# Three groups of instructions moved in a fused attention and experts kernel: the residual into y, half of the scores, a bias centring

## The chip, the cores and the metric

The kernel runs on one core of a Trainium2 chip. The metric is the device time of one execution in microseconds (us). Each engine (TensorE or PE, VectorE or DVE, ScalarE or ACT, GpSimd or Pool, SyncE or SP) has its own list of instructions, written out by hand, which it runs in that order; semaphores tie the lists together.

## What is computed

Input x is 4 sequences of 32 tokens by 256 features, 128 tokens in all. Three stages follow, each on a layer-normed x and each added back to x:

```
x = x + xattn(layernorm(x), ctx)     # cross attention, 16 heads of 16, causal, context of 64 features
x = x + attn(layernorm(x))           # self attention, 16 heads of 16, q/k/v/o = x W + b + 0.5 (x B) A
x = x + ffn(layernorm(x))            # mixture of experts

def attn:  scores = q k / 4;  p = softmax(scores);  out = lora_linear(p v, Wo, bo, Bo, Ao)
def ffn:   logits = x @ router_w.T;  s = sqrt(softplus(logits))
           4 best of 32 experts by s + expert_bias, weights s / sum(s)
           out = sum over the experts of weight * (silu(clip(x wg)) * clip(x wu)) @ wd, + one shared expert
```

All 32 experts are computed for all 128 tokens, and the router's weights (zero for those not chosen) scale them. Everything is float32.

## The kernel before, in words

The 128 tokens fill the 128 partitions. D = 256 features are two chunks of 128 (DC = 2, index c), so heads 0 to 7 are chunk 0 and heads 8 to 15 are chunk 1. The work goes through three stretches.

**Layer 1 and layer 2 (attention).** In the helpers, a = 0 is the cross attention ("layer 1") and a = 1 the self attention ("layer 2"). For a chunk c, the steps are: `project_T(which, c, ...)` (L361) makes k (which 0) or q (which 1), transposed, in PSUM bank pair `bP[c]`; VectorE spreads k over a head mask (`spread_keys`, L806) and ScalarE copies q out (L705); `scores(a, c)` (L388) makes 16 small matmul passes, and each of its eight products counts `scores_ready` up by one; VectorE finds the row maximum and subtracts it (`shift_half`, L811 and L813); ScalarE takes the exponential (`exp_half`, L641); TensorE transposes the result (`transpose_probs`, L395), which VectorE copies out for chunk 0 (L819) and ScalarE for chunk 1 (L652); `attend(a, c)` (L402) multiplies with v; VectorE normalises (`normalise_heads`, L845 and L847), TensorE transposes the heads (`transpose_heads`, L409), and they are multiplied by the output weights into two forms: y in `bY` (`add_to_y`, L413) and its transpose in `bXT` (`add_to_xt`, L417). The residual x comes into `bY` by a matmul of x with the identity (L467), which opens that accumulation and may run once ScalarE has read LoRA's v part out of the same bank (`lora_v_ready`, L656). v of layer 2 is made by `values_part` (L370) in two halves of two sequences each, one ahead of `scores(1, 1)` and one behind it; ScalarE copies it out with `copy_v` (L647) and VectorE with its own (L824), two quarters each.

The statistics of y (L874, L795, L798 on VectorE) give a variance, and Pool raises it to the power -0.5 (`inverse_sqrt(n)`, L314) for layer norm n = 1 and 2. `bo_centred` (L326, 128 by 2 elements on Pool) is the output bias with its mean taken off; its first reader is ScalarE's `xfT` copy (L722), in front of the experts.

**The routing.** After layer 2, `inverse_sqrt(2)` gives rstd; then a chain of small steps on ScalarE and VectorE (L731 to L959) ends in `gate`, the router's weights.

**The experts.** There are 16 pairs of experts. For all but the first two (WHOLE) pairs, the weights of a pair are split in a high and a low part: ScalarE writes the high part (`gu_high(p)`, L664, whole, or `gu_high_chunk(p, c)`, L669, half), Pool subtracts it from the weights to give the low part (`gu_low(p, c)`, L333, one per half pair), and TensorE multiplies with both (L561). Of the last eight down projections the same is done at L763 and L345. Pool's order, by hand: `inverse_sqrt(1)`, `bo_centred`, nine `gu_low`, `inverse_sqrt(2)`, a wait for `gate`, nineteen `gu_low`, eight L345. ScalarE's order in layer 2: q copy 0, q copy 1 (L705), `gu_high(WHOLE + 2)` (L664), `exp_half(1, 0)`, `copy_v(0)`, `exp_half(1, 1)`, `copy_v(1)`, probsT copy (L652), `gu_high(WHOLE + 3)`.

SP's list loads all weights; its loads for pair 8 and later wait for `gu_lo_ready`, that is for Pool's `gu_low` of the pair whose buffer they reuse.

Of the kernel before, what the change touches and what calls it, by code (L numbers as in the profile page):

```python
# [56 lines left out]
def raw_slot(p):  # L57
    return p if p < RAW else (p + WHOLE) % RAW


def build(nc, x, consts, mask, small, ctx_kv, x_wq, lora, rows, attn_w, shared_w, moe_w, out):
    with ExitStack() as ctx:  # L62
        def sb(name, shape, dt=F32):
            return ctx.enter_context(nc.sbuf_tensor(name, shape, dt))
# [7 lines left out]
        def sem(name):  # L72
            return ctx.enter_context(nc.semaphore(name))
# [17 lines left out]
        def dn_part(i, w):  # L91

            at = i % 2 * 2 * D
            return gu_w[:, (FIRST + i // 2) % SLOTS, w, at:at + 2 * D]
# [17 lines left out]
        xnT = sb("xnT", [128, DC, T])  # L112
# [76 lines left out]
        q_psum = sem("q_psum")  # L189
# [106 lines left out]
        @block.gpsimd  # L296
        def _(pool):
            nc.gpsimd.memset(minus_mean[:], -1.0 / D).then_inc(powers_set, 1)
            nc.gpsimd.memset(inv_sqrt_power[:], -0.5).then_inc(powers_set, 1)
            nc.gpsimd.memset(ln_floor[:], 2.0 ** -64).then_inc(powers_set, 1)  # L300
            nc.gpsimd.memset(v_heads[:], 0.0).then_inc(zeroed, 1)
            nc.gpsimd.memset(key[:, E:E + K], SENTINEL).then_inc(zeroed, 1)
            nc.gpsimd.memset(score2[:, E:E + 1], 2e-20).then_inc(zeroed, 1)
            pool.wait_ge(zeroed, 3)
            for j in range(G):

                nc.gpsimd.memset(v_heads[j * S:(j + 1) * S, :, :, j, HD], 1.0).then_inc(zeroed, 1)
            pool.wait_ge(zeroed, 3 + G)

            pool.wait_ge(powers_set, 3)  # L310

            def inverse_sqrt(n):
                pool.wait_ge(var_ready, n + 1)
                nc.gpsimd.tensor_tensor(rstd[:, n:n + 1], var_eps[:, n:n + 1], inv_sqrt_power[:], ALU.pow  # L314
                                        ).then_inc(rstd_ready[n], 1)

            inverse_sqrt(0)
            pool.wait_ge(ld["aw_vo"], 16)
            for c in range(DC):
                cols = slice(c * D, (c + 1) * D)  # L320
                pool.wait_ge(lora_v_ready, c + 1)
                nc.gpsimd.tensor_tensor(aw_sb[:, 2, cols], aw_sb[:, 2, cols], lora_v[:, c], ALU.add  # L322
                                        ).then_inc(v_merged, 1)
            inverse_sqrt(1)
            pool.wait_ge(bo_mean_ready, 1)
            nc.gpsimd.tensor_scalar(bo_centred[:], consts_sb[:, BIASO:BIASO + DC], bo_mean[:, 0:1], bo_mean[:, 1:2],  # L326
                                    ALU.add, ALU.add).then_inc(bo_ready, 1)

            def gu_low(p, c):

                pool.wait_ge(gu_hi_ready, DC * (p - WHOLE) + c + 1)
                cols = slice(c * GU, (c + 1) * GU)
                nc.gpsimd.tensor_tensor(gu_w[:, p % SLOTS, 1, cols], gu_raw[:, raw_slot(p), cols],  # L333
                                        gu_w[:, p % SLOTS, 0, cols], ALU.subtract).then_inc(gu_lo_ready[c], 1)

            for p in range(WHOLE, PAIRS):
                for c in range(DC):
                    if (p, c) == (WHOLE + 4, 1):
                        inverse_sqrt(2)
                        pool.wait_ge(gate_ready, 1)  # L340
                    gu_low(p, c)
            for i in range(LAST):
                pool.wait_ge(dn_hi_ready, i + 1)
                at = (FIRST + i) * 2 * D
                nc.gpsimd.tensor_tensor(dn_part(i, 1), dn_w[:, at:at + 2 * D], dn_part(i, 0), ALU.subtract  # L345
                                        ).then_inc(dn_lo_ready, 1)

        @block.tensor
        def _(pe):
            aw = [aw_sb[:, m].rearrange("p (c n) -> p c n", c=DC) for m in range(4)]  # L350
# [7 lines left out]
            def project_T(which, c, w, x_t, done, biased=False):  # L358

                for k in range(DC):  # L360
                    last = nc.tensor.matmul(bP[c][:, which, 0:T], w[:, k, c * 128:(c + 1) * 128], x_t[:, k, :],  # L361
                                            start=(k == 0 and not biased), stop=(k == DC - 1), skip_group_check=biased)
                last.then_inc(done, 1)
# [13 lines left out]
            def scores(a, c):  # L377

                for g in range(2):
                    r = slice(64 * g, 64 * g + 64)  # L380
                    if a == 0:

                        nc.tensor.matmul(bP[c][:, g, 0:128], mask_sb[:, 0:128], mask_sb[:, 128:],
                                         start=True, stop=False, skip_group_check=True)
                for b in range(B):
                    for g in range(2):
                        r = slice(64 * g, 64 * g + 64)
                        nc.tensor.matmul(bP[c][b * S:(b + 1) * S, g, 0:G * S], qT[r, a, c, b * S:(b + 1) * S],  # L388
                                         k_heads[r, c, :, b * S:(b + 1) * S],
                                         start=(a == 1), stop=True, skip_group_check=True).then_inc(scores_ready, 1)  # L390
# [8 lines left out]
            def attend(a, c):  # L399
                for g in range(2):  # L400
                    for b in range(B):
                        last = nc.tensor.matmul(bP[c][b * S:(b + 1) * S, 1, g * G * V1:(g + 1) * G * V1],  # L402
                                                probsT[:, c, g, b * S:(b + 1) * S], v_heads[:, b, 2 * c + g],
                                                start=True, stop=True, skip_group_check=True)
                last.then_inc(pv_ready, 1)

            def transpose_heads(a, c):
                pe.wait_ge(heads_ready, 2 * a + c + 1)
                nc.tensor.transpose(bP[c][:, 0, 0:T], heads_out[:, a, c * 128:(c + 1) * 128], ident  # L409
                                    ).then_inc(headsT_psum, 1)  # L410
# [51 lines left out]
            attend(0, 0)  # L462
            pe.wait_ge(probsT_act_ready, 1)
            attend(0, 1)
            transpose_heads(0, 0)
            pe.wait_ge(lora_v_ready, DC)
            nc.tensor.matmul(bY[:, 0:D], ident, x_sb[:], start=True, stop=False, skip_group_check=True)  # L467
            transpose_heads(0, 1)
            pe.wait_ge(ld["small"], 16)
            pe.wait_ge(headsT_ready, 1)  # L470
# [34 lines left out]
            project_T(0, 0, aw[0], xnT, k_psum, biased=True)  # L505
            project_T(1, 0, aw[1], xnT, q_psum)
            project_T(0, 1, aw[0], xnT, k_psum, biased=True)
            project_T(1, 1, aw[1], xnT, q_psum)
            pe.wait_ge(q_ready, DC + 1)
            pe.wait_ge(k_ready, DC + 1)  # L510
            scores(1, 0)
            pe.wait_ge(lora_merged, 5)
            pe.wait_ge(v_merged, DC)
            values_part(range(B // 2))
# [546 lines left out]
```

## Time and profile before

| what | value |
|---|---|
| device time, median of 3 runs | 74.0 us (73.44 to 74.24) |
| the profiled execution, device time | 74.25 us |
| its span, first to last instruction | 72.0 us |
| PE / DVE / ACT / POOL busy | 67.0 / 44.9 / 43.8 / 50.4 us |
| x16 loads of expert weights, 512 KB each | 8.1 us to land, the median |

The profile tells of one execution; times in it count from its span's start. 2.25 us of the device time lie around the span. "Busy" is the time in which an engine had an instruction of the program in work; TensorE's ends are modelled, so that its share says little on whether it is the bound. What is read here is who waits for whom.

### The profile page before, as it was taken

Reading aid. Unit: us, or ns where it says so; the run is one execution under the profiler, and the core shown is the slowest. Engines: PE = TensorE matmul, PEld = TensorE weight load, DVE = VectorE, ACT = ScalarE, POOL = GpSimd, SP = SyncE. Lnnn points to the kernel's source line nnn. Section 1 sums busy time; section 2 is a strip of 40 time slices with the busy share of each in tenths; the row PEclk is TensorE's granted clock in tenths of the full one; section 3 lists DMA queues with packets and bytes.
Section 4 is the critical chain, followed back from the end, with each engine's and each line's share of the span. In section 5 each row is a group of like instructions: output and inputs, shape, how many; then the busy total and the mean of one; then the engine's idle time right before and its main releaser. Section 6 shows DMA issues by size and latency. Waiting matters only on the chain.

```text
span 72.0 us, 1593 instructions
## 1 busy us (share of the span) xinstructions
PE 67.0 (93%) x558; PEld 50.5 (70%) x560; DVE 44.9 (62%) x127; ACT 43.8 (61%) x95; POOL 50.4 (70%) x56
## 2 busy tenths in 40 slices
PE   5999997998998999999998999999999999999850
PEld 2347664797864495657777888888888788899740
DVE  0058487784788536698999935743763685698220
ACT  0603647659488656559999999651456876774200
POOL 7330005249999798000799999999999999999900
PEclk9999999999999999999999999999999999999999
DMA  0899999999999999999747799910000000000002
GB/s 4 277 275 291 371 420 378 274 393 417 417 407 396 383 399 328 392 381 383 295 96 248 263 364 360 392 63 0 9 0 0 0 0 0 0 0 0 0 0 73
DMA packets 6342, 15.74 MB, mean 219 GB/s; under 512 B 704, under 2 KB 1472, under 8 KB 6336
## 3 DMA queue, kind: packets, MB, share of 16 engines
q1 hardware_dynamic: 6048, 15.39, 59.4%
q10 hardware_dynamic: 288, 0.27, 1.1%
q8 instruction: 4, 0.07, 0.3%
q14 instruction: 2, 0.02, 0.1%
HBM read 15.52 MB, written 0.13 MB: 218 GB/s over the span
## 4 chain that ended last, share of the span: by engine, by line
POOL 51%; PE 25%; DVE 12%; ACT 4%; issue 2%; POOLq 2%; DVEq 0%
POOL gu_w L333 38%; POOL gu_w L345 12%; PE bE L424 6%; PE bP L361 4%; PE bP L388 2%; DVE shifted L813 2%; DVE gu_clip L917 2%; POOLq L62 2%; DVE row_max L811 2%; PE bP L430 2%; PE bY L413 1%; ACT gu_w L664 1%; PE bY L591 1%; ACT probs L641 1%; PE bP L395 1%
## 5 line engine op out<-in xcount | busy, mean ns | idle before, releaser
L333 POOL TENSOR_TENSOR gu_w<-gu_raw,gu_w 128x512 fp32r<-128x512 f32 x28 | 34.9, 1285 | 6.2 <-DVE gate L959 5.8
L561 PE MATMUL bP<-gu_w,xnT_parts 128*128 128x512 f32 x66 | 19.0, 422 | 0.0
L917 DVE TENSOR_SCALAR gu_clip<-bP,clip_at 128x512 f32<-128x512 f32 x13 | 10.4, 808 | 7.3 <-PE bP L561 7.3
L561 PEld LDWEIGHTS bP<-gu_w,xnT_parts 128*128 128x128 f32 x66 | 12.3, 188 | 2.9 <-issue 0.5
L664 ACT ACTIVATE gu_w<-gu_raw 128x1024 fp32r<-128x1024 f32 x11 | 11.5, 1050 | 0.1
L345 POOL TENSOR_TENSOR gu_w<-dn_w,gu_w 128x512 fp32r<-128x512 f32 x8 | 10.0, 1294 | 0.0
L583 PE MATMUL bY<-dn_w,hT 128*128 128x256 f32 x32 | 8.2, 380 | 0.0
L970 DVE SCALAR_TENSOR_TENSOR h<-gu_clip,gate,bP 128x128 f32<-128x128 f32 x26 | 7.8, 340 | 0.0
L591 PE MATMUL bY<-gu_w,hT_parts 128*128 128x256 f32 x48 | 7.4, 294 | 0.3 <-POOL gu_w L345 0.3
L591 PEld LDWEIGHTS bY<-gu_w,hT_parts 128*128 128x128 f32 x48 | 6.2, 189 | 0.5 <-POOL gu_w L345 0.5
L573 PE MATMUL bXT<-consts_sb,h 128*128 128x128 f32 x33 | 6.3, 275 | 0.2 <-DVE h L970 0.2
L757 ACT ACTIVATE hT<-bXT 128x256 f32<-128x256 f32 (+1 forms) x9 | 3.3, 363 | 4.8 <-PE bXT L573 4.8
L751 ACT ACTIVATE bP<-gu_clip,rstd 128x256 f32<-128x256 f32 x13 | 6.0, 470 | 0.0
L573 PEld LDWEIGHTS bXT<-consts_sb,h 128*128 128x128 f32 x33 | 4.3, 140 | 2.3 <-DVE h L970 0.6
L322 POOL TENSOR_TENSOR aw_sb<-aw_sb,lora_v 128x256 f32<-128x256 f32 x2 | 1.4, 728 | 6.4 <-ACT lora_v L656 6.4
L583 PEld LDWEIGHTS bY<-dn_w,hT 128*128 128x128 f32 x32 | 5.5, 190 | 0.4
L424 PE MATMUL bE<-const-bfloat16-1.0 128*128 128x512 bf16 x12 | 5.0, 565 | 0.8 <-PEq L1054 0.8
L757 ACT ACTIVATE hT_parts<-bXT 128x256 fp32r<-128x256 f32 x8 | 3.1, 385 | 4.2 <-PE bXT L573 4.2
L561 PE MATMUL bE<-gu_w,xnT_parts 128*128 128x512 f32 x18 | 5.1, 416 | 0.0
L314 POOL TENSOR_TENSOR rstd<-var_eps,inv_sqrt_power 128x1 f32<-128x1 f32 x3 | 1.8, 599 | 4.6 <-DVE var_eps L798 4.6
L763 ACT ACTIVATE gu_w<-dn_w 128x512 fp32r<-128x512 f32 x8 | 4.6, 624 | 0.0
L547 PE MATMUL bP<-gu_raw,xfT 128*128 128x512 f32 x8 | 4.0, 602 | 0.0
(149 smaller groups left out, 106.1 us busy)
## 6 DMA issues: line engine op xcount, KB each, us to landing
gu_raw<-moe_w_dram SPq DMA_DIRECT2D x16, 512.0 KB, 8.1
dn_w<-moe_w_dram SPq DMA_DIRECT2D x16, 256.0 KB, 6.2
aw_sb<-attn_w_dram SPq DMA_DIRECT2D x2, 512.0 KB, 7.1
shared_sb<-shared_w_dram SPq DMA_DIRECT2D x1, 384.0 KB, 14.7
small_sb<-small_dram SPq DMA_DIRECT2D x1, 370.0 KB, 6.9
xwq_sb<-x_wq_dram SPq DMA_DIRECT2D x1, 256.0 KB, 3.5
lora_sb<-lora_dram SPq DMA_DIRECT2D x1, 256.0 KB, 4.6
ctx_sb<-ctx_kv_dram ACTq DMA_DIRECT2D x1, 192.0 KB, 3.1
```

The lines of the kernel that those rows point to most:

```text
L333: nc.gpsimd.tensor_tensor(gu_w[:, p % SLOTS, 1, cols], gu_raw[:, raw_slot(p), cols], gu_w[:, p % SLOTS, 0, cols], ALU.subtract).then_inc(g ...
L345: nc.gpsimd.tensor_tensor(dn_part(i, 1), dn_w[:, at:at + 2 * D], dn_part(i, 0), ALU.subtract).then_inc(dn_lo_ready, 1)
L424: nc.tensor.matmul(bank, ones, ones_wide, start=True, stop=True, skip_group_check=True)
L561: last = nc.tensor.matmul(bGU[n % 5][:, 0:GU], xnT_parts[:, a, k, :], gu_w[:, (n - 1) % SLOTS, w, k * GU:(k + 1) * GU], start=(k == 0 and ...
L573: last = nc.tensor.transpose(bHT[n % 2][:, e * T:(e + 1) * T], h[:, n % 4, e, :], ident)
L583: last = nc.tensor.matmul(bY[:, 0:D], hT[:, n % 3, e, :], dn_w[:, at:at + D], start=False, stop=False, skip_group_check=True)
L591: last = nc.tensor.matmul(bY[:, 0:D], hT_parts[:, n % 3, a, e, :], dn_part(i, w)[:, e * D:(e + 1) * D], start=False, stop=(n == PAIRS and ...
L664: nc.scalar.activation(gu_w[:, p % SLOTS, 0], gu_raw[:, raw_slot(p)], ACT.Copy).then_inc(gu_hi_ready, DC)
L751: nc.scalar.activation(dst, gu_clip[:, n % 4, 0:width, 0, :], ACT.Silu, scale=rstd[:, 2:3]).then_inc(silu_ready, 1)
L757: nc.scalar.activation(dst, bHT[n % 2][:, 0:width * T], ACT.Copy).then_inc(hT_ready, 1)
L917: nc.vector.tensor_scalar(gu_clip[:, n % 4, 0:width], bank[:, 0:width * 2 * I], clip_at[:, 0:1], clip_at[:, 1:2], ALU.min, ALU.max).then_i ...
L970: last = nc.vector.scalar_tensor_tensor(h[:, n % 4, e], gu_clip[:, n % 4, e, 1, :], weight_e, bank[:, e * 2 * I:e * 2 * I + I], ALU.mult, ...
```

## The change

Three groups of instructions change their place; none is added or taken away.

```diff
@@ gpsimd (Pool) @@
                 nc.gpsimd.tensor_tensor(aw_sb[:, 2, cols], aw_sb[:, 2, cols], lora_v[:, c], ALU.add
                                         ).then_inc(v_merged, 1)
-            inverse_sqrt(1)
             pool.wait_ge(bo_mean_ready, 1)
             nc.gpsimd.tensor_scalar(bo_centred[:], consts_sb[:, BIASO:BIASO + DC], bo_mean[:, 0:1], bo_mean[:, 1:2],
                                     ALU.add, ALU.add).then_inc(bo_ready, 1)
+            inverse_sqrt(1)
@@ tensor (PE) @@
             attend(0, 0)
             pe.wait_ge(probsT_act_ready, 1)
             attend(0, 1)
-            transpose_heads(0, 0)
             pe.wait_ge(lora_v_ready, DC)
             nc.tensor.matmul(bY[:, 0:D], ident, x_sb[:], start=True, stop=False, skip_group_check=True)
+            transpose_heads(0, 0)
             transpose_heads(0, 1)
@@ tensor (PE) @@
             project_T(0, 0, aw[0], xnT, k_psum, biased=True)
             project_T(1, 0, aw[1], xnT, q_psum)
             project_T(0, 1, aw[0], xnT, k_psum, biased=True)
-            project_T(1, 1, aw[1], xnT, q_psum)
             pe.wait_ge(q_ready, DC + 1)
             pe.wait_ge(k_ready, DC + 1)
             scores(1, 0)
+            project_T(1, 1, aw[1], xnT, q_psum)
             pe.wait_ge(lora_merged, 5)
             pe.wait_ge(v_merged, DC)
             values_part(range(B // 2))
```

In words: (A) in layer 1 the residual's matmul runs ahead of both head transposes instead of between them; (B) in layer 2 the scores of chunk 0 run ahead of the projection of q's chunk 1 instead of behind it; (C) Pool centres the bias ahead of `inverse_sqrt(1)` instead of behind it.

## Rows read from the trace of the kernel before

**Rows 1.** The page: the span, TensorE's granted clock, the chain by engine.
```profile
span 72.0 us, 1593 instructions
...
PEclk9999999999999999999999999999999999999999
...
POOL 51%; PE 25%; DVE 12%; ACT 4%; issue 2%; POOLq 2%; DVEq 0%
```

**Rows 2.** Timeline of Pool: start us, us, engine, line, operation, count, idle before.
```profile
15.45 0.55 POOL L314 TENSOR_TENSOR rstd<-var_eps,inv_sqrt_power 128x1 f32<-128x1 f32 x1 [2.42 <-DVE var_eps L798]
16.00 0.38 POOL L326 TENSOR_SCALAR bo_centred<-consts_sb,bo_mean 128x2 f32<-128x2 f32 x1
16.33 7.44 POOL L333 TENSOR_TENSOR gu_w<-gu_raw,gu_w 128x512 fp32r<-128x512 f32 x6
24.18 3.73 POOL L333 TENSOR_TENSOR gu_w<-gu_raw,gu_w 128x512 fp32r<-128x512 f32 x3 [0.40 <-ACT gu_w L664]
28.15 0.68 POOL L314 TENSOR_TENSOR rstd<-var_eps,inv_sqrt_power 128x1 f32<-128x1 f32 x1 [0.25 <-DVE var_eps L798]
34.65 23.72 POOL L333 TENSOR_TENSOR gu_w<-gu_raw,gu_w 128x512 fp32r<-128x512 f32 x19 [5.82 <-DVE gate L959]
```

**Rows 3.** The chain of waits in order of time, its end: start us, us.
```profile
68.41 0.98 PE bY L591 x6
```

**Rows 4.** Timeline of TensorE's weight loads (PEld), projections to attend of layer 2.
```profile
17.22 1.86 PEld L361 LDWEIGHTS bP<-xnT,aw_sb 128*128 128x128 f32 x16 [0.40 <-DVE xnT L884]
19.20 0.18 PEld L388 LDWEIGHTS bP<-k_heads,qT 64*32 64x32 f32 x16
19.58 0.49 PEld L370 LDWEIGHTS bE<-aw_sb,xnT 128*32 128x32 f32 x32 [0.20 <-issue]
20.17 0.18 PEld L388 LDWEIGHTS bP<-k_heads,qT 64*32 64x32 f32 x16
...
23.20 0.54 PEld L402 LDWEIGHTS bP<-v_heads,probsT 128*32 128x32 f32 x32 [0.53 <-ACT v_heads L647]
```

**Rows 5.** Timeline of ScalarE in the same stretch.
```profile
18.42 0.37 ACT L705 ACTIVATE qT<-bP,small_sb 128x128 f32<-128x128 f32 x1 [0.49 <-PE bP L361]
19.31 0.37 ACT L705 ACTIVATE qT<-bP,small_sb 128x128 f32<-128x128 f32 x1 [0.53 <-PE bP L361]
19.58 1.05 ACT L664 ACTIVATE gu_w<-gu_raw 128x1024 fp32r<-128x1024 f32 x1
20.86 0.42 ACT L641 ACTIVATE probs<-shifted 128x256 f32<-128x256 f32 x1 [0.23 <-DVE shifted L813]
```

**Rows 6.** Timeline of VectorE in the same stretch.
```profile
17.97 0.69 DVE L806 TENSOR_TENSOR k_heads<-bP,consts_sb 128x512 f32<-128x512 f32 x1 [0.80 <-PE bP L361]
...
19.94 0.42 DVE L811 TENSOR_REDUCE row_max<-bP 128x8 f32<-128x256 f32 x1 [0.39 <-PE bP L388]
...
20.91 0.42 DVE L811 TENSOR_REDUCE row_max<-bP 128x8 f32<-128x256 f32 x1
...
21.81 0.43 DVE L819 COPY probsT<-bP 128x256 f32<-128x256 f32 x1
22.26 0.86 DVE L824 COPY v_heads<-bE 32x256 f32<-32x256 f32 x2
```

**Rows 7.** Timeline of layer 1's end: ScalarE, TensorE and its weight loads.
```profile
11.85 0.38 ACT L656 ACTIVATE lora_v<-bY 128x256 f32<-128x256 f32 x1
...
12.56 0.33 PE L409 MATMUL bP<-consts_sb,heads_out 128*128 128x128 f32 x1
...
12.73 0.60 PE L467 MATMUL bY<-x_sb,consts_sb 128*128 128x256 f32 x2
...
13.11 0.14 PEld L409 LDWEIGHTS bP<-consts_sb,heads_out 128*128 128x128 f32 x1 [0.18 <-DVE heads_out L847]
...
13.47 0.28 ACT L691 ACTIVATE heads_outT<-bP 128x128 f32<-128x128 f32 x1 [0.27 <-PE bP L409]
...
13.80 0.30 PEld L413 LDWEIGHTS bY<-small_sb,heads_outT 128*128 128x128 f32 x2 [0.18 <-ACT heads_outT L691]
```

## Prediction
> **What bounds the kernel now.** I read the page first (span, clock, chain by engine), then the chain of waits from its end backwards, then the timeline of each engine around the three edits.
>
> The chain that ended last is half Pool [rows 1]. It ends with 0.98 us of matmuls after Pool's last subtraction [rows 3]; before that, Pool runs its subtractions without a pause from 34.65 [rows 2]. It starts there because it waited 5.82 us for `gate`, the end of the routing, which begins with `inverse_sqrt(2)` at 28.15 [rows 2]. So all that lies behind 28.15 is a fixed length as seen from here, about 43.9 us of the span's 72.0, and what an edit is worth is how far it moves the start at 28.15. Two things could hold that start: VectorE's variance of layer 2, or Pool itself, with its nine early `gu_low`. Pool was idle 0.25 us before it, released by VectorE [rows 2]. So the attention path sets it, and Pool has 0.25 us to spare.
>
> In layer 2 I therefore follow the attention path from 17.22. TensorE runs nearly without a pause: 16 projection passes, scores of chunk 0 from 19.20, half of v from 19.58, scores of chunk 1 from 20.17 [rows 4]. VectorE finds maxima from 19.94 and from 20.91, copies the transposed probabilities from 21.81 and two quarters of v from 22.26 to 23.12; `attend` begins at 23.20, right behind them [rows 4, 6]. The path is a close race of engines, and the reader should see the small slacks: ScalarE finished `gu_high` (19.58 + 1.05 = 20.63) 0.23 us before the exponential of chunk 0 could start at 20.86 [rows 5]. That 0.23 us decides part B.
>
> **Part B, scores of chunk 0 ahead of q's projection 1.** Nothing is added; TensorE's work up to `scores(1, 1)` is the same.
>
> What gets earlier: the scores need q 0, copied by 18.42 + 0.37 = 18.79 [rows 5], and k 0, ready at 17.97 + 0.69 = 18.66 [rows 6]. With 0.05 us from a releaser to TensorE's load (13.47 + 0.28 = 13.75, load at 13.80 [rows 7]) they start at 18.84 instead of 19.20, 0.36 us earlier. Their maximum started 0.74 us after their load both times (19.20 to 19.94, 20.17 to 20.91 [rows 4, 6]), so now at 19.58; VectorE's second k spread ends about there. The shifted scores are ready 0.36 us earlier.
>
> What gets later: q's projection 1. The trace before does not show a projection behind scores. It shows v behind scores: its load came 0.38 us after the scores' first load, of which 0.20 is idle with no releaser [rows 4]. I take the same 0.38 here, since it is the nearest row: load at 19.22. From the first load of a projection to its reader took 17.97 - 17.22 = 0.75 us when it was not running on from another one [rows 4, 6]. So ScalarE starts q copy 1 at 19.97 instead of 19.31, 0.66 us later.
>
> What is queued behind that copy on ScalarE: `gu_high(WHOLE + 2)`, 0.27 us after it (19.31 to 19.58), 1.05 us long, and only then the exponential of chunk 0 [rows 5]. It now runs 20.24 to 21.29, and the exponential starts at about 21.25 (between 21.19, if it overlaps the end as `gu_high` overlaps the q copy by 0.10, and 21.31, if it doesn't). That is 0.39 us later than 20.86, though its input is ready 0.36 us earlier: the gain is lost and the slack of 0.23 overdrawn. Then the probabilities' transpose and VectorE's copy (21.81 before) start 0.39 later, for that copy begins as soon as the transpose behind the exponential is through; it started 0.95 behind it before (20.86 to 21.81), with no idle noted of VectorE's [rows 5, 6]. The v copies and `attend` follow: `attend` at 23.59 instead of 23.20 [rows 4, 6].
>
> The other half: v starts about 0.55 to 0.64 us behind the projection's load at 19.22 (four passes 0.11 apart, first gap wider, perhaps a second switch of shape), takes 0.59 (19.58 to 20.17), so `scores(1, 1)` start near 20.41, 0.24 later [rows 4]; q 1 is ready at 19.97 + 0.37 + 0.05 = 20.39, so it fits. Its maximum comes at 21.15 instead of 20.91 [rows 6], and its exponential and what follows 0.24 later too. That is less than 0.39, so it does not arrive last. B costs 0.39 us. The bounds: below, no switch cost behind the scores (0.20 less) and a first pass that is prefetched (0.10 less), with the overlap on ScalarE, gives 0.39 - 0.20 - 0.10 - 0.06 = 0.03; above, a second idle of 0.20 of the same kind on TensorE gives 0.6.
>
> By the Trainium skill (TensorE: Matmul & The Clock Gate, "The mechanism" in Part 3) weights are pulled ahead of matmuls in flight only if their row groups do not conflict or they go to the background buffer, and (same page, phase 5 in Part 2) back-to-back matmuls follow each other at the length of their columns. By the second sentence alone the projection would follow without the 0.20, and B would cost about 0.13 to 0.19; the first, with loads of 128 rows behind loads of 64, would give an idle such as the 0.20 of [rows 4]. The measured idle decides.
>
> **Part A, the residual ahead of both transposes.** It is two passes of 0.22 each (12.73 to 13.33 for both with the drain). It waits for `lora_v`, ready at 11.85 + 0.38 = 12.23, ahead of the first transpose's 12.56, for which TensorE waited [rows 7]. I estimate that it runs from about 12.35 to 12.8. So the first transpose goes from 12.56 to about 12.78, and its reader comes some 0.16 later. The second is bound by its input: load at 13.11, idle before it released by `heads_out`, and a lone transpose takes 0.33, so its end stays at 13.44 and ScalarE's copy at 13.47 [rows 7]. The product for chunk 1, which waits for that copy (13.80), ends y. The product for chunk 0 starts some 0.1 later and then touches it: I take +0.05, between -0.03 (only the second transpose's queueing gone) and +0.10. Everything behind y moves by that.
>
> **Part C, the bias ahead of `inverse_sqrt(1)`.** `bo_centred` (0.38 us) goes into Pool's idle 2.42 us before 15.45 [rows 2], since ScalarE writes `bo_mean` ahead of its lora_v copy of 11.85 [rows 7]. `gu_low` then starts at 16.00 instead of 16.33. The first six end 0.33 earlier, at 23.44, but the seventh waits for ScalarE's `gu_high(WHOLE + 3)` anyway (0.40 idle before 24.18 [rows 2]). The time goes into that wait, so C is worth nothing; at most the loads for pairs 8 and 9 start 0.33 earlier. If the cover were gone, it would be worth 0.33 only if Pool held `inverse_sqrt(2)`, which it doesn't. B makes ScalarE's `gu_high(WHOLE + 2)` end at 21.29, 0.35 after Pool wants it (16.00 + 4 x 1.24 = 20.96), which C's 0.33 pays; the sixth still ends at about 23.8, before 24.18.
>
> **The sum.** 0.39 + 0.05 + 0 = +0.44 us. Span 72.0 to 72.44; the profiled execution 74.25 to 74.69. It lies 0.25 above the median of 74.0, so on the median the forecast is 74.4 us, +0.6%. Runs of this kernel spread by 0.8 us, so about 1% (0.74 us) is what a measurement can tell from no change.
>
> **Rivals.**
> 1. The projection follows the scores without idle. B is then 0.39 - 0.20 = 0.19, or 0.13 with the overlap of 0.06 on ScalarE, middle 0.16. Sum 0.16 + 0.05 = +0.2: 74.2 us. For it: sixteen loads of the scores take 0.18 in all [rows 4]. Against it: 0.20 of idle where v follows scores [rows 4]. It is what the skill's back-to-back rule, cited above, would give.
> 2. The 0.36 us of part B reach the end. This needs the exponential of chunk 0 not to be held by `gu_high` and `scores(1, 1)` not to be later: -0.36 + 0.05 = -0.3: 73.7 us. Against it: the maximum of chunk 1 came at 20.91 with VectorE free at about 20.83 (two operations of 0.42 from 19.94), so even a free first half leaves TensorE as the bound [rows 6].
> 3. Slower by more than 1%: the granted clock falls. It stayed at full in all 40 slices [rows 1] though TensorE waited 0.53 us before `attend` [rows 4]. B lengthens the waits between 20.6 and 23.6 by 0.39. If it fell from 2.4 to 1.2 GHz there, TensorE's work in the 4.95 us from `attend` at 23.20 to `inverse_sqrt(2)` at 28.15 [rows 2, 4] would take twice as long. With TensorE on half of that stretch it is 2.5 us: 74.4 + 2.5 = 76.9 us. It decides from 0.3 us on (0.44 + 0.3 = 0.74). Against it: the keep-busy matmuls stay where they are.
>
> **How the numbers follow.** Forecast as worked out: 0.5. Rival 1: 0.2. Rival 2: 0.12, rival 3: 0.05; 0.13 for what I don't see, of both signs. The first two lie within 0.74 us of 74.0 except where the forecast meets its upper bound (0.6 + 0.10 = 0.7) and an unlucky spread. Slower by over 1%: 0.05 + 0.10 from that bound + 0.04 = 0.19. Faster by over 1%: 0.03 of rival 2 and 0.07 unseen = 0.10. Within 1%: 0.71. The range: bounds 0.0 to +0.7 on 74.0, and the spread of single runs around them (-0.5, +0.3), 73.5 to 75.0.
>
> **What would show it.** In the trace after: scores L388 load near 18.84; q copy 1 on ScalarE near 19.97 (rival 1: 19.75); the exponential L641 of chunk 0 near 21.25 and with no idle released by VectorE before it; VectorE now waiting for TensorE before L819; `attend` near 23.6; `inverse_sqrt(2)` near 28.6, still released by VectorE's variance; Pool idle before its seventh `gu_low` still. Shown wrong if the projection follows the scores without a gap, or if `inverse_sqrt(2)` comes earlier than 28.15.

## The result and the profile after

The changed kernel takes 74.45 us (median of 21 runs) against 73.7 us for the kernel before (21 runs beside them): a ratio of 1.0081, 95% interval 1.0055 to 1.0107. So it is 0.6 us slower, give or take 0.2, where the forecast was 0.44 us. The medians are of all 21 executions, of which a few in each kernel are about 2 us longer; the ratio compares the others alone. The profiled execution has a span of 72.5 us against 72.0.

The page of the kernel after, span and chain by engine:

```profile
span 72.5 us, 1595 instructions
...
PEclk9999999999999999999999999999999999999999
...
POOL 51%; PE 26%; DVE 10%; ACT 5%; issue 2%; POOLq 2%; DVEq 0%
```

Pool still holds the end and TensorE's clock is still granted in full in each slice [rows 1]. Pool's timeline says where the difference came in:

```profile
13.04 0.38 POOL L325 TENSOR_SCALAR bo_centred<-consts_sb,bo_mean 128x2 f32<-128x2 f32 x1
15.74 0.56 POOL L314 TENSOR_TENSOR rstd<-var_eps,inv_sqrt_power 128x1 f32<-128x1 f32 x1 [2.31 <-DVE var_eps L798]
16.26 4.97 POOL L333 TENSOR_TENSOR gu_w<-gu_raw,gu_w 128x512 fp32r<-128x512 f32 x4
21.64 2.50 POOL L333 TENSOR_TENSOR gu_w<-gu_raw,gu_w 128x512 fp32r<-128x512 f32 x2 [0.41 <-ACT gu_w L664]
24.73 3.72 POOL L333 TENSOR_TENSOR gu_w<-gu_raw,gu_w 128x512 fp32r<-128x512 f32 x3 [0.59 <-ACT gu_w L664]
28.73 0.68 POOL L314 TENSOR_TENSOR rstd<-var_eps,inv_sqrt_power 128x1 f32<-128x1 f32 x1 [0.28 <-DVE var_eps L798]
35.22 23.71 POOL L333 TENSOR_TENSOR gu_w<-gu_raw,gu_w 128x512 fp32r<-128x512 f32 x19 [5.81 <-DVE gate L959]
```

`inverse_sqrt(1)` is 0.29 us later than in [rows 2] (15.74 to 15.45) and `inverse_sqrt(2)` 0.58 us later (28.73 to 28.15). From there to the restart at 35.22 it is 6.49 us, before 6.50. So about half of the loss lies in layer 1, half in layer 2, and none behind. Pool's gain from part C is seen too: `bo_centred` at 13.04, and then two waits for ScalarE's high parts, 0.41 and 0.59, where there was one of 0.40.

Layer 1, timeline of the kernel after (TensorE, its weight loads, ScalarE):

```profile
12.41 0.70 PE L466 MATMUL bY<-x_sb,consts_sb 128*128 128x256 f32 x2
...
12.94 0.52 PE L409 MATMUL bP<-consts_sb,heads_out 128*128 128x128 f32 x2
...
...
13.25 0.53 ACT L691 ACTIVATE heads_outT<-bP 128x128 f32<-128x128 f32 x2 [1.00 <-PE bP L409]
...
13.64 0.73 PEld L413 LDWEIGHTS bY<-small_sb,heads_outT 128*128 128x128 f32 x4 [0.37 <-issue]
...
13.67 1.10 PE L413 MATMUL bY<-small_sb,heads_outT 128*128 128x256 f32 x4 [0.21 <-ACT heads_outT L691]
```

The first transpose goes at 12.94, not at 12.56 [rows 7], and the four passes of y's products start at 13.64 and run in one piece, where before they were two pairs with the second at 13.80.

Layer 2, weight loads of TensorE, two rows of its matmuls, then ScalarE, then VectorE:

```profile
17.50 1.41 PEld L361 LDWEIGHTS bP<-xnT,aw_sb 128*128 128x128 f32 x12 [0.39 <-DVE xnT L884]
19.11 0.19 PEld L388 LDWEIGHTS bP<-k_heads,qT 64*32 64x32 f32 x16 [0.20 <-ACT qT L705]
19.50 0.52 PEld L361 LDWEIGHTS bP<-xnT,aw_sb 128*128 128x128 f32 x4 [0.20 <-issue]
20.14 0.49 PEld L370 LDWEIGHTS bE<-aw_sb,xnT 128*32 128x32 f32 x32
20.72 0.18 PEld L388 LDWEIGHTS bP<-k_heads,qT 64*32 64x32 f32 x16
...
23.78 0.54 PEld L402 LDWEIGHTS bP<-v_heads,probsT 128*32 128x32 f32 x32 [0.56 <-ACT v_heads L647]
```

```profile
19.11 0.45 PE L388 MATMUL bP<-k_heads,qT 64*32 64x128 f32 x16
19.50 0.71 PE L361 MATMUL bP<-xnT,aw_sb 128*128 128x128 f32 x4
```

```profile
20.25 0.37 ACT L705 ACTIVATE qT<-bP,small_sb 128x128 f32<-128x128 f32 x1 [1.19 <-PE bP L361]
20.51 1.05 ACT L664 ACTIVATE gu_w<-gu_raw 128x1024 fp32r<-128x1024 f32 x1
21.46 0.40 ACT L641 ACTIVATE probs<-shifted 128x256 f32<-128x256 f32 x1
```

```profile
19.85 0.42 DVE L811 TENSOR_REDUCE row_max<-bP 128x8 f32<-128x256 f32 x1
20.31 0.42 DVE L813 TENSOR_TENSOR shifted<-bP,row_max 128x256 f32<-128x256 f32 x1
21.46 0.42 DVE L811 TENSOR_REDUCE row_max<-bP 128x8 f32<-128x256 f32 x1 [0.73 <-PE bP L388]
21.92 0.42 DVE L813 TENSOR_TENSOR shifted<-bP,row_max 128x256 f32<-128x256 f32 x1
22.39 0.42 DVE L819 COPY probsT<-bP 128x256 f32<-128x256 f32 x1
```

Set against [rows 4 to 6], with each time counted from the first projection's load (17.22 before, 17.50 after), since all of layer 2 is shifted by 0.28:

| event in layer 2, us after the first projection's load | before | after |
|---|---|---|
| row maximum of chunk 0 (VectorE) | 2.72 | 2.35 |
| exponential of chunk 0 (ScalarE) | 3.64 | 3.96 |
| row maximum of chunk 1 (VectorE) | 3.68 | 3.96 |
| `attend(1, 0)` (TensorE) | 5.98 | 6.29 |

The maximum of chunk 0 is 0.37 us earlier and everything else 0.3 us later. ScalarE's exponential has no idle in front of it: it comes straight out of `gu_high`.

### The profile page after: what moved, and what is told of

It reads as the page before. It is cut to its first block, busy times and chain, and to the rows that moved or that the text cites. A ratio compares the mean times of both kernels' runs of the same rounds, so it can differ in the third digit from the quotient of the medians.

```text
span 72.5 us, 1595 instructions
## 1 busy us (share of the span) xinstructions
PE 67.7 (93%) x560; PEld 50.8 (70%) x560; DVE 44.9 (62%) x127; ACT 43.7 (60%) x95; POOL 50.4 (70%) x56
## 2 busy tenths in 40 slices
DMA packets 6342, 15.74 MB, mean 217 GB/s; under 512 B 704, under 2 KB 1472, under 8 KB 6336
## 4 chain that ended last, share of the span: by engine, by line
POOL 51%; PE 26%; DVE 10%; ACT 5%; issue 2%; POOLq 2%; DVEq 0%
POOL gu_w L333 38%; POOL gu_w L345 12%; PE bE L424 6%; PE bP L361 5%; PE bP L388 2%; DVE shifted L813 2%; DVE gu_clip L917 2%; POOLq L62 2%; DVE row_max L811 2%; PE bP L430 2%; PE bY L413 2%; ACT gu_w L664 1%; PE bY L591 1%; ACT probs L641 1%; PE bP L395 1%
```

## The experiments

**How intervals are read.** Executions differ in layer 1 by more than the edits change: the `attend(0, 1)` load, up to which all kernels here are the same program, lies between 10.98 and 12.03, and at 13.55 in pair_only. The start of TensorE's first work on the context (L430) is one part, at 4.15 in c_alone and 4.68 in the kernel before. TensorE's pace is another: the eight projection passes of layer 1 (L361) took 1.15 us in the kernel before and 2.07 in pair_only, though both pages show the granted clock as full. The span of one profile therefore tells little of an edit of 0.1 to 0.3 us. Intervals between two events inside an execution do: I use three, from `attend(0, 1)`'s load to the first projection's load of layer 2 (interval 1), from there to `attend(1, 0)`'s load (interval 2), and from there to `inverse_sqrt(2)` (interval 3), which was 4.95 in all. The fourth, from `inverse_sqrt(2)` to the end, was 43.75 to 43.81 in all.

| kernel | interval 1 | interval 2 | ratio of times to before, 95% |
|---|---|---|---|
| before | 5.22 | 5.98 | |
| after | 5.46 | 6.29 | 1.0081 (1.0055 to 1.0107) |
| a_alone | 5.46 | 5.97 | 1.0039 (0.9990 to 1.0087) |
| b_alone | 5.48 | 6.29 | 1.0025 (0.9978 to 1.0071) |
| c_alone | 5.29 | 5.98 | 1.0006 (0.9959 to 1.0053) |
| b_guhigh | 5.21 | 6.15 | 1.0027 (0.9990 to 1.0065) |
| a_split | 5.25 | 5.98 | 1.0002 (0.9967 to 1.0037) |
| a_split_open | 5.25 | 5.98 | one run |
| pair_v | 5.22 | 5.87 | 0.9963 (0.9933 to 0.9993) |
| pair_only | 5.22 | 5.98 | one run |
| chunk_late | 5.22 | 5.98 | 1.0005 (0.9960 to 1.0051) |
| both_late | 5.22 | 5.87 | 0.9957 (0.9918 to 0.9996) |
| both_late_again | 5.22 | 5.86 | 1.0016 (0.9974 to 1.0058) |

**Each part alone.** The edits are the three hunks of the change's diff, one at a time.

Part A alone:

> Only part A of the change. Theory 1 (A holds the product for chunk 0): the first head transpose queues behind the residual, its copy comes 0.3 us later, and since y's four product passes run back to back from there, y and all behind it move by the same: inverse_sqrt(2) at 28.4, span and time +0.25 us (+0.3%). Rival (the forecast's +0.05): the second transpose's copy holds y, so the time is +0.05 us, below what can be told, and the 0.28 us seen in the trace after belongs to B or to the execution.

Interval 1 rose from 5.22 to 5.46, interval 2 stayed. Its weight loads:

```profile
11.86 0.28 PEld L402 LDWEIGHTS bP<-v_heads,probsT 128*32 128x32 f32 x16 [0.27 <-ACT probsT L652]
...
13.48 0.73 PEld L413 LDWEIGHTS bY<-small_sb,heads_outT 128*128 128x128 f32 x4 [0.37 <-issue]
...
17.33 1.86 PEld L361 LDWEIGHTS bP<-xnT,aw_sb 128*128 128x128 f32 x16 [0.40 <-DVE xnT L884]
```

The kernel before, weight loads, ScalarE's first copy and the passes of y's products, not among the rows above:

```profile
12.01 0.28 PEld L402 LDWEIGHTS bP<-v_heads,probsT 128*32 128x32 f32 x16 [0.27 <-ACT probsT L652]
...
12.93 0.28 ACT L691 ACTIVATE heads_outT<-bP 128x128 f32<-128x128 f32 x1 [0.70 <-PE bP L409]
...
13.32 0.30 PEld L413 LDWEIGHTS bY<-small_sb,heads_outT 128*128 128x128 f32 x2
...
13.35 1.15 PE L413 MATMUL bY<-small_sb,heads_outT 128*128 128x256 f32 x4
```

From `attend(0, 1)` to the first product it is 13.48 - 11.86 = 1.62 us, before 13.32 - 12.01 = 1.31. A costs 0.24 us, and the time's ratio, +0.39%, agrees but by itself tells neither 0.05 from 0.25 nor either from nothing.

Part B alone:

> Only part B. The two parts of the change lie one behind the other on the path, so they should add: theory 1 says +0.30 us (+0.4%), q copy 1 on ScalarE at 19.97, attend at 23.50. The forecast's own term was +0.39. Rival: A and B overlap or feed each other, and B alone costs all of +0.58 or nothing.

Interval 2 is 6.29, as in the kernel after, with A absent: +0.31 us. The parts add: 0.24 + 0.31 = 0.55, beside 0.58 at `inverse_sqrt(2)`, of which 0.02 is a later `attend(0, 1)` (12.03 to 12.01). But interval 1 was 5.48 here without part A, which was not expected. The rows of ScalarE and VectorE show why:

```profile
15.37 0.63 ACT L669 ACTIVATE gu_w<-gu_raw 128x512 fp32r<-128x512 f32 x1 [1.12 <-DMA gu_raw<-moe_w_dram]
15.91 0.26 ACT L695 ACTIVATE xcT<-bXT 128x128 f32<-128x128 f32 x1
...
16.25 0.42 DVE L884 TENSOR_TENSOR xnT<-xcT,bY 128x256 f32<-128x256 f32 x1 [0.39 <-ACT xcT L695]
```

This execution reached `attend(0, 1)` at 11.25, 0.76 us earlier than the one of before, and then `gu_high_chunk(WHOLE + 1, 0)` waited 1.12 us for its load with the xcT copy queued behind it; VectorE waited 0.39 us for that copy before it made xnT, the input of the projections. The head start was partly lost again. That is a property of the kernel, not of part B: c_alone, which has no part B, shows it too (below, with chunk_late).

Part C alone:

> Only part C. Theory: zero. Pool's first gu_low starts at 16.00 instead of 16.33 and the idle before the seventh grows from 0.40 to 0.73 us; inverse_sqrt(2) stays at 28.15. Rival: Pool is nearer to the path than its 0.25 us of idle says, and the time falls by up to 0.25 us (-0.3%).

Interval 2 and interval 3 are those of before. Pool:

```profile
23.22 3.72 POOL L333 TENSOR_TENSOR gu_w<-gu_raw,gu_w 128x512 fp32r<-128x512 f32 x3 [0.83 <-ACT gu_w L664]
27.19 0.68 POOL L314 TENSOR_TENSOR rstd<-var_eps,inv_sqrt_power 128x1 f32<-128x1 f32 x1 [0.25 <-DVE var_eps L798]
```

The wait before the seventh `gu_low` is 0.83 instead of 0.40 (0.73 was expected), and that before `inverse_sqrt(2)` is 0.25 as before: what C frees is waited away. Its span of 70.9 us is no gain of C's: layer 1 had started 1.0 us earlier (`attend(0, 1)` at 10.98), and the timed runs give 1.0006.

**What in part B costs: b_guhigh.** B, and on ScalarE:

```diff
             for c in range(DC):
+                if c == 1:
+                    gu_high(WHOLE + 2)
                 act.wait_ge(q_psum, DC + c + 1)
                 ... q copy c ...
-            gu_high(WHOLE + 2)
```

> Part B, with ScalarE's gu_high(WHOLE + 2) moved from behind q copy 1 into the wait in front of it. Theory S (ScalarE's queue is what made B cost): the exponential of chunk 0 starts at about 20.5, B's cost falls to zero or below. Theory T (TensorE's second half holds VectorE as well, nearly a tie with ScalarE): the exponential of chunk 0 starts at 20.5 too, but scores(1, 1) stay 0.27 us late, VectorE's maximum of chunk 1 with them, and B still costs about 0.25 us (+0.3%).

ScalarE:

```profile
18.49 1.05 ACT L664 ACTIVATE gu_w<-gu_raw 128x1024 fp32r<-128x1024 f32 x1
19.77 0.37 ACT L707 ACTIVATE qT<-bP,small_sb 128x128 f32<-128x128 f32 x1 [0.24 <-PE bP L361]
20.30 0.42 ACT L641 ACTIVATE probs<-shifted 128x256 f32<-128x256 f32 x1 [0.16 <-DVE shifted L814]
```

VectorE:

```profile
20.99 0.42 DVE L812 TENSOR_REDUCE row_max<-bP 128x8 f32<-128x256 f32 x1 [0.72 <-PE bP L388]
...
21.79 0.42 DVE L820 COPY probsT<-bP 128x256 f32<-128x256 f32 x1
```

The projections began at 17.03, so the exponential of chunk 0 came at 3.27 instead of 3.96, now really ahead of before's 3.64. The maximum of chunk 1 stayed at 3.96, held 0.72 us by TensorE's scores. Interval 2 is 6.15: of B's 0.31, ScalarE's queue accounts for 0.14, and 0.17 remain, with VectorE held by TensorE's second half and then running on without idle to its copy. Theory S alone falls, theory T holds in kind, though its 0.25 was too much. VectorE's start of the shifting of chunk 1 and of the copy behind it tell the sizes: here they are 0.34 apart (21.45 to 21.79), with no wait for the transpose, in the kernel after 0.47 (21.92 to 22.39) and in the kernel before 0.44 (21.37 to 21.81). So the second half had 0.10 us to spare before, which leaves about 0.18 of its 0.28, and in the kernel after the first half held the copy by another 0.13.

**What in part A costs: a_split and a_split_open.**

```diff
-            transpose_heads(0, 0)
             pe.wait_ge(lora_v_ready, DC)
-            nc.tensor.matmul(bY[:, 0:D], ident, x_sb[:], start=True, stop=False, skip_group_check=True)
+            nc.tensor.matmul(bY[:, 0:128], ident, x_sb[:, 0:128], start=True, stop=False, skip_group_check=True)
+            transpose_heads(0, 0)
+            nc.tensor.matmul(bY[:, 128:D], ident, x_sb[:, 128:D], start=True, stop=False, skip_group_check=True)
```

> A half dose of part A: the residual's first 128 columns ahead of the first head transpose, its other 128 between the transposes, where all of it stood before. Theory 1 (what A costs is the time by which the residual holds the first transpose and so the product for chunk 0): half the length ahead, so the interval from attend(0, 1)'s load to the first projection's load is between 5.21 us (before) and 5.47 us (A), at most 5.34; the time is +0.05 to +0.13 us. Rival (the order itself costs, a wait on lora_v or the bank, whatever the length): 5.47 as with A.

This kernel leaves out something: each half opens the accumulation, and the residual's first 128 columns are missing from the output. The instructions and their lengths are those of the next kernel, whose output is whole and whose intervals are the same, so its times can be used.

Interval 1 is 5.25: +0.03 instead of A's +0.24. So neither the order nor the wait on `lora_v` costs by itself. Timeline of a_split:

```profile
11.31 0.28 PEld L402 LDWEIGHTS bP<-v_heads,probsT 128*32 128x32 f32 x16 [0.27 <-ACT probsT L653]
...
12.71 0.73 PEld L413 LDWEIGHTS bY<-small_sb,heads_outT 128*128 128x128 f32 x4 [0.16 <-issue]
```

The first product came 12.71 - 11.31 = 1.40 us after `attend(0, 1)`, 0.09 later than before, and y 0.03 later; in A it came 0.31 later, and y 0.24. So the first product had about 0.06 us to spare, and what is beyond is lost in full: 0.31 - 0.06 = 0.25. That is the price of A, read from these two kernels. The passes of y's products say the same: in the kernel before, with the wait for the second copy among them, they span 1.15 us (from 13.35), and in the kernel after 1.10 in one piece (from 13.67), so that wait cost only 0.05. The whole residual moved the first product by 0.31 and its half by 0.09; the 0.22 between them is the length of half the residual, one of its two passes of 0.22. The beginning costs less, since the residual's load comes 0.37 us behind `attend(0, 1)` (11.68 in a_split), in time that TensorE spent waiting for the heads before (transpose at 12.56 - 12.01 = 0.55).

a_split_open changes the second half's flag to start=False:

> a_split with one flag changed: the second half of the residual no longer opens its accumulation (start=False). In a_split each half opened it, and the first half of the residual was missing from the output; if the opening of one matmul clears the marks of the whole bank, the second half here finds its columns cleared by the first and writes them fresh, and the output is whole. Same instructions and lengths: the interval from attend(0, 1) to the projections is 5.21 to 5.26 us as in a_split. Rival: the marks are cleared only for the columns written, then the second half adds to what LoRA's v part left in the bank.

The interval is again 5.25, and the output is whole. Columns 128 to 255 had held LoRA's v part, and a matmul that doesn't open wrote them afresh: opening an accumulation in columns 0 to 127 of the bank cleared the marks, which decide whether a matmul adds or writes afresh, of columns 128 to 255 as well.

**The other direction: pair_v and pair_only.** If TensorE's second half holds, it should come earlier, not the first half. On TensorE, and for pair_v on VectorE too:

```diff
-            pe.wait_ge(lora_merged, 5)
-            pe.wait_ge(v_merged, DC)
-            values_part(range(B // 2))
             pe.wait_ge(q_ready, DC + 2)
             pe.wait_ge(k_ready, DC + 2)
             scores(1, 1)
-            values_part(range(B // 2, B)).then_inc(v_psum, 1)
+            pe.wait_ge(lora_merged, 5)
+            pe.wait_ge(v_merged, DC)
+            values_part(range(B)).then_inc(v_psum, 1)
@@ vector, pair_v alone @@
-            copy_probsT(1)
             dve.wait_ge(v_psum, 2)
             copy_v(2, bE)
             copy_v(3, bE).then_inc(v_dve_ready, 1)
+            copy_probsT(1)
```

> The other way round: the kernel before, with scores(1, 1) ahead of all of v instead of in its middle, and VectorE's v copies ahead of its copy of the transposed probabilities. TensorE changes tile shape twice less, each seen to cost 0.20 us of idle. If TensorE's second half holds layer 2, as b_guhigh showed, the interval from the first projection's load to attend falls from 5.98 to about 5.88 us and the time by 0.1 us (-0.1%); attend is then held by VectorE's copies, which is why it is not more. Rival: the first half's exponential and transpose hold, nothing is gained (5.98).

> pair_v with VectorE's copies in the order of before: only scores(1, 1) ahead of v. Theory: the maximum of chunk 1 comes at 3.52 us after the first projection instead of 3.68, as in pair_v, but VectorE then waits for the transposed probabilities of chunk 0, whose exponential stays at 3.64, so attend stays at 5.95 to 5.98: both edits are needed, and the first half's exponential is the next thing that holds. Rival: TensorE's order alone gave the 0.11 us, attend at 5.87.

VectorE in pair_v:

```profile
20.39 0.41 DVE L810 TENSOR_REDUCE row_max<-bP 128x8 f32<-128x256 f32 x1
20.84 0.42 DVE L812 TENSOR_TENSOR shifted<-bP,row_max 128x256 f32<-128x256 f32 x1
21.30 0.87 DVE L823 COPY v_heads<-bE 32x256 f32<-32x256 f32 x2
22.20 0.42 DVE L818 COPY probsT<-bP 128x256 f32<-128x256 f32 x1
```

VectorE in pair_only:

```profile
22.74 0.42 DVE L812 TENSOR_TENSOR shifted<-bP,row_max 128x256 f32<-128x256 f32 x1
23.35 0.43 DVE L818 COPY probsT<-bP 128x256 f32<-128x256 f32 x1 [0.19 <-PE bP L395]
```

In both the maximum of chunk 1 comes at 3.52 (before 3.68). Its scores load at 19.38 in pair_v, 2.51 us after the first projection instead of 2.95, but VectorE is at work on chunk 0 until its maximum of chunk 1 begins at 20.39, so only 0.16 of the gain is left. In pair_only VectorE then waits for the transposes of chunk 0 and interval 2 stays at 5.98; in pair_v it copies v meanwhile, and the interval is 5.87. TensorE's order alone gains nothing, as was expected. VectorE's order alone was not run. An estimate: in pair_v `attend` loads at 22.74, 2.35 us after the maximum of chunk 1 began (20.39); in the kernel before that would be 20.91 + 2.35 = 23.26, no earlier than its 23.20 [rows 4, 6]. So it looks as if both edits are needed. This is the opposite of part B's idea: what was worth moving, by 0.11 us, is the second half.

**A wait for a load in layer 1: chunk_late, both_late, both_late_again.**

```diff
-            gu_high_chunk(WHOLE + 1, 0)
             act.wait_ge(xt_psum, 1)
             nc.scalar.activation(xcT[:, 0], bXT0[:, 0:T], ACT.Copy).then_inc(xt0_ready, 1)
+            gu_high_chunk(WHOLE + 1, 0)
```

> The kernel before, with ScalarE's gu_high_chunk(WHOLE + 1, 0) behind its xcT copy instead of ahead of it. In b_alone and c_alone, whose first layer ran 0.8 to 1.0 us earlier, that chunk waited for its load and held the xcT copy. Theory: in an execution that starts early the interval from attend(0, 1) to the projections is 5.13 to 5.21 instead of 5.29 and 5.48, in one that starts late 5.21 as before; the time falls by up to 0.1 us. Rival: the interval stays at 5.29 or more in an early execution, so another wait for a load holds it.

The profiled execution reached `attend(0, 1)` at 11.12, early, and interval 1 was 5.22, where b_alone and c_alone had 5.48 and 5.29. But this execution doesn't put the edit to the test. ScalarE's `gu_high(WHOLE)` ended at 13.71 + 1.06 = 14.77, and the semaphore events of the trace have the chunk's load landed at 14.74. In the old order the xcT copy would have started at about 15.3 instead of 15.21 (an estimate), and xnT, which follows such a copy by 0.34 in b_alone and c_alone, began at 15.87 anyway.

What shows the held copy is the traces of b_alone (above) and of c_alone, where it was the whole `gu_high(WHOLE)` that waited for its load, with the chunk and the xcT copy right behind it:

```profile
13.83 1.06 ACT L664 ACTIVATE gu_w<-gu_raw 128x1024 fp32r<-128x1024 f32 x1 [1.10 <-DMA gu_raw<-moe_w_dram]
...
15.79 0.42 DVE L884 TENSOR_TENSOR xnT<-xcT,bY 128x256 f32<-128x256 f32 x1 [0.20 <-ACT xcT L695]
```

VectorE's own xcT copy began at 15.57 in b_alone and 15.30 in c_alone, and in the kernel before xnT began 0.43 behind it (16.32 to 16.75). Without the wait xnT would have begun at 16.00 and 15.73, which is 0.25 and 0.06 earlier and brings both intervals to 5.23. The timed runs show no difference (1.0005, interval 0.9960 to 1.0051). Whether the edit helps in an execution that has the wait, and how often that is, stays open.

> pair_v and chunk_late together. If both work, -0.1 to -0.2 us (-0.2%) against the kernel before. If neither does, the same time.

> both_late measured once more, on another job, against the kernel before: -0.11 us of layer 2 and up to 0.26 us in those executions in which ScalarE's chunk would have waited for its load; ratio 0.995 to 0.998.

Interval 2 was 5.87 and 5.86. The ratios were 0.9957 and, measured again, 1.0016; their intervals overlap. pair_v alone gave 0.9963, with an interval that leaves out 1. A gain of 0.11 us (0.15%) in layer 2 is shown by the interval; that any of these kernels is faster than the kernel before in the timed runs is not settled. Against the changed kernel, pair_v and both_late are 0.24 + 0.31 + 0.11 = 0.66 us shorter by the intervals.

## Why the prediction was right, and where it was off

The forecast was 74.4 us, +0.44, within 1% at the highest chance; it came to 74.45 us and +0.6, which is 0.8% with an interval that reaches 1.07%. Direction and bound were right: `inverse_sqrt(2)` moves, the length behind it is fixed (43.8), and Pool isn't what holds it. The place was right in part: layer 1 was to bear 0.05 of the 0.44 and bore 0.24 of 0.55. That the two times, 74.4 and 74.45, nearly meet is luck: the forecast stood on a median of 74.0 of 3 executions, and the 21 beside the changed kernel gave 73.7.

- **Part B, forecast +0.39, measured +0.31.** The path was as forecast: scores 0.37 earlier (0.36), q copy 1 at 19.97 when the shift of layer 1 is taken off (20.25 - 0.28), a pause of 0.20 in the weight loads behind the scores, the exponential out of `gu_high` at 3.96. The forecast exponential (21.25, that is 4.03 after 17.22) was 0.07 late: ScalarE's exponential overlaps `gu_high`'s end by 0.10 (21.46 against 20.51 + 1.05 = 21.56), the lower of the two bounds named. The step "less than 0.39, so it does not arrive last" held, but it hid how near the other half was: forecast +0.24, measured +0.28, beside ScalarE's +0.32. b_guhigh showed it: with ScalarE out of the way 0.17 of the 0.31 remained. Reading the end of one route as the cause would have suggested a repair that brings back less than half.
- **Part A, forecast +0.05 (bound +0.10), measured +0.24.** This is the term that was mis-sized, beyond its own bound. The failing step is "the first transpose goes from 12.56 to about 12.78, and its reader comes some 0.16 later ... the product for chunk 0 starts some 0.1 later". The residual's load came at 12.41, not 12.35; the transpose's pass at 12.94; its reader at 13.25, 0.32 later; and the product at 13.64, 0.32 later. I had treated the second copy (13.75) as what holds y, since the chunk 1 product waited for it. But the wait for it cost y only 0.05 (passes of 1.15 against 1.10 in one piece): once the first product is that late, the passes run in one piece and the first sets the end. a_alone and a_split show the two ends of it.
- **Part C, forecast 0, measured 0.** The freed 0.33 went into waits for ScalarE, as forecast: in the kernel after the fifth `gu_low` waited 0.41 for B's later `gu_high` (0.35 forecast), and the seventh still waited 0.59.
- **Rival 1**, a projection that follows the scores without idle, is refuted in its size: the projection's load came 0.39 behind the scores' first load (19.11 to 19.50), as forecast (0.38). But the 0.20 is a pause of the weight loads, not of TensorE: by the rows of the matmuls, whose ends are modelled, the scores run from 19.11 to 19.56 and the projection's begin at 19.50. So the trace doesn't stand against the Trainium skill's back-to-back rule (TensorE: Matmul & The Clock Gate, phase 5 in Part 2), which is about matmuls; what erred was to apply it to the sixteen short loads. Nor does it bear out its sentence on row groups (the same page, "The mechanism" in Part 3) as the reason for the pause. In the kernel before, layer 1's v has loads of 64 rows (6.18 + 0.49) and the projection's loads of 128 rows follow at 6.76, 0.09 later; behind layer 1's scores loads of 16 rows pause for 0.20 (8.68 + 0.18 to 9.06). The pause goes with the scores, whichever group follows, and not with the change of height. What in the scores makes it was not tested.
- **Rival 2**, B's gain reaches the end: it reached the maximum of chunk 0 and no further; even in b_guhigh, where the exponential was earlier too, the interval was longer than before.
- **Rival 3**, the clock: granted in full in all slices, and the last scores' sixteen loads ahead of `attend` take 0.18 in both kernels.

The errors of A (-0.19) and B (+0.08) are of opposite sign and partly cancel, which is luck too; the sum was 0.11 short of the intervals' 0.55, well within the range.

## What to carry to other kernels

Work moved ahead on a first half is worth nothing if the second half pays for it: look at what is queued behind each delayed reader on its engine, and compute both halves to their join, for a near-tie means that the repair of one gives back only part. When a consumer runs several passes in a row, the input of the first can hold its end as well as the input of the last: compare the first's slack with the length of what is moved ahead of it. For edits of some tenths of a microsecond, intervals between two events of an execution repeat to 0.01 or 0.02 us, as long as nothing in them waits for a load (interval 1 of b_alone and c_alone did), where the times of whole runs need dozens.

## What the hardware showed that was not expected

- The accumulation marks of a PSUM bank: with a second opening (start=True) on other columns of the bank, the first half of the residual was missing from the output; with the second half not opening, it was whole. The opening cleared marks beyond its own columns. That agrees with the Trainium skill (PSUM — Partial Sum Buffer, "The four PSUM rules"), by which the whole bank is cleared; here it is shown for 256 of its 512 columns.
- The row maximum started 0.74 us after the scores' first load in before and after (19.20 to 19.94, 20.72 to 21.46), though their sixteen loads take 0.18. In this kernel it held wherever VectorE was free, so it can be used as a duration.
- Intervals 3 and 4 were equal within 0.06 us over thirteen profiles, while the `attend(0, 1)` of layer 1 moved by up to 2.6 us. Part of that is TensorE at about half its pace in the first microseconds (2.07 us against 1.15 for the same eight passes), which the granted clock on the page doesn't show.
